# A graph-network pair kernel with 122 instead of 109 edge chunks sorted by cell, and the added source rows moved from TensorE to VectorE

## The reference, cut to what matters

```
h = relu(layernorm(x1 @ W1 + b1) * g1 + bt1)
edge_weights = sigmoid(relu(concat(h[src], h[dst]) @ We1 + be1) @ We2 + be2)
aggr = segment_sum(edge_weights[:, None] * h[src], dst, 6250)
gate = sigmoid(concat(h, aggr) @ Wg + bg)
out = layernorm(x1 + layernorm(gate * aggr + (1 - gate) * h) * g2 + bt2)
```

## Time and profile before

| | |
|---|---|
| median of 3 runs | 2032.33 us (2027.09 to 2037.23) |
| the profiled execution's own time | 2030.64 us |
| its span | 2028.9 us |
| mean granted TensorE clock | 0.905 |
| busy: PE / PEld / DVE / ACT / POOL | 87% / 69% / 77% / 66% / 68% |
| edge stage, node stage | 0 to 363 us, 363 to 524 us |
| gather stage: 26 steps without riders, 190 with | 524 to 785 us, 785 to 1937 us |
| end stage | 1937 to 2029 us |

### The profile page before, as it was taken

How to read it: one execution, slowest core, us unless ns; L and a number is a source line. 1 busy time by engine, 2 the same in 40 slices (tenths; PEclk the granted TensorE clock), 3 DMA queues, 4 the chain that set the end, 5 groups by cost and what they waited for, 6 DMA issues and landing times.

```text
span 2028.9 us, 42803 instructions
## 1 busy us (share of the span) xinstructions
PE 1762.4 (87%) x13262; PEld 1398.9 (69%) x13263; DVE 1560.1 (77%) x4602; ACT 1338.8 (66%) x3369; POOL 1375.0 (68%) x1415
## 2 busy tenths in 40 slices
PE   3899998667687789999999999999999999989880
PEld 2787777555465556666777778878887888778750
DVE  7877887596899657777788877778877887767766
ACT  1565555475655206778888878788877887767635
POOL 4564741167677777777777777777777777777736
PEclk9999998789678859898999999999998999999985
DMA  7898998415544455666666666777666677767502
GB/s 272 278 306 289 329 313 294 154 42 197 174 130 137 142 157 166 177 178 190 189 198 193 190 209 200 208 204 215 197 209 196 198 213 212 212 188 213 148 11 64
DMA packets 293551, 395.44 MB, mean 195 GB/s; under 512 B 73153, under 2 KB 195780, under 8 KB 293195
## 3 DMA queue, kind: packets, MB, share of 16 engines
q1 hardware_dynamic: 236559, 240.51, 37.6%
q0 software_dynamic: 54144, 147.92, 25.2%
q10 hardware_dynamic: 2620, 4.25, 0.6%
HBM read 377.32 MB, written 15.17 MB: 193 GB/s over the span
## 4 chain that ended last, share of the span: by engine, by line
PE 51%; POOL 24%; issue 11%; DVE 8%; DMA 3%; DVEq 1%; SPq 1%; ACT 1%; ACTq 0%; POOLq 0%
POOL x_rows L998 14%; PE psum L531 10%; PE psum L581 6%; PE psum L565 6%; POOL late_gathers L998 5%; POOL ring L998 5%; PE psum L1494 4%; PE psum L1495 4%; PE psum L1529 4%; PE psum L1506 4%; PE psum L1382 2%; PE psum L1537 2%; PE psum L560 2%; DVE stats L1869 1%; PE psum L1412 1%
## 5 line engine op out<-in xcount | busy, mean ns | idle before, releaser
L998 POOL DMA_INDIRECT x_rows<-src_table,lane_src x680 | 656.5, 966 | 216.0 <-issue 204.7
L585 DVE TENSOR_TENSOR sums<-sums,psum 128x128 f32 (+3 forms) x822 | 207.0, 252 | 181.2 <-issue 115.1
L576 DVE TENSOR_SCALAR weighted<-iota,lane_dst,weight 128x40 f32<-128x40 f32 x1128 | 262.4, 329 | 17.3 <-ACT weight L1205 17.2
L998 POOL DMA_INDIRECT late_gathers<-src_table,lane_src x224 | 217.0, 969 | 68.3 <-issue 67.6
L998 POOL DMA_INDIRECT ring<-src_table,lane_src x224 | 215.4, 962 | 68.3 <-issue 67.6
L531 PE MATMUL psum<-ring 128*64 128x128 f32 x3128 | 225.4, 288 | 35.3 <-issue 30.2
L565 PE MATMUL psum<-x_rows,ident 128*128 128x512 f32 x340 | 198.3, 677 | 46.0 <-DMA x_rows<-src_table,lane_src 46.0
L570 DVE SCALAR_TENSOR_TENSOR psum<-psum,we_all 128x512 f32<-128x512 f32 (+1 forms) x216 | 187.0, 866 | 50.5 <-PE psum L565 50.5
L531 PEld LDWEIGHTS psum<-ring 128*64 128x64 f32 x3128 | 177.6, 142 | 60.7 <-issue 42.8
L1217 ACT ACTIVATE sums<-psum 128x512 f32<-128x512 f32 (+1 forms) x149 | 87.4, 587 | 172.7 <-PE psum L1495 172.2
L572 DVE TENSOR_REDUCE logit<-psum 128x4 f32<-128x512 f32 (+1 forms) x216 | 184.6, 855 | 16.6 <-issue 0.8
(11 more groups left out here) (266 smaller groups left out, 3887.2 us busy)
## 6 DMA issues: line engine op xcount, KB each, us to landing
ring<-in_edge_attr SPq DMA_DIRECT2D x195, 512.0 KB, 5.3
ring<-cell_table SPq DMA_DIRECT2D x145, 256.0 KB
ring<-rel_table SPq DMA_DIRECT2D x70, 512.0 KB
ring<-src_table SPq DMA_DIRECT2D x192, 128.0 KB
x_rows<-src_table,lane_src POOLq DMA_INDIRECT x680
ring<-dst_table SPq DMA_DIRECT2D x282, 32.0 KB
ring<-src_table SPq DMA_DIRECT2D x106, 64.0 KB
src_table<-ring SPq DMA_DIRECT2D x12, 512.0 KB, 2.9
```

The costliest lines, as they stand in the source:

```text
L576: last = eng.tensor_scalar(out[:, j, :], iota1[:, 0:W], dst[:, j:j + 1], wt[:, j:j + 1], ALU.is_equal, ALU.mult)
L585: return eng.tensor_tensor(table[..., bass.ds(start, width)], table[..., bass.ds(start, width)], part, ALU.add)
L998: eng.indirect_dma_start(gathered(c)[:, j, :], None, src_table, bass.IndirectOffsetOnAxis(ap=lane_src[:, t:t + 1], axis=0)).then_inc(gathe ...
```

## The change

Thirteen more chunks (109 to 121) are sorted, as a sixth class with cap 2; 25 more riders follow from it (174 in all). The sort steps of classes 2 to 5 take 3 edge columns in place of 2. In every step with a rider (`vector_adds`), TensorE's `hidden_sum` does nothing; VectorE adds the gathered rows to the hidden rows in PSUM itself, ahead of L570. One of the three `place_dst` tiles is dropped, and `weigh_` waits with `PLACES` = 2. `far_onehot3` becomes a view of `node_hot`, and two PSUM result areas move.

```diff
-CLASSES = ((0, 41, 4), (41, 19, 2), (60, 19, 2), (79, 16, 2), (95, 14, 2))
+CLASSES = ((0, 41, 4), (41, 19, 2), (60, 19, 2), (79, 16, 2), (95, 14, 2), (109, 13, 2))
 
-SPANS = (80, 96, P, P, P)
-SORTED = 109
+SPANS = (80, 96, P, P, P, P)
+SORTED = 122
...
-        far_onehot3 = sb("far_onehot3", [P, J, WP], BF16)
...
-        SORT_STEPS = [9] + [2] * (n_classes - 1)
+        SORT_STEPS = [9, 2, 3, 3, 3, 3]
...
-        later_tiles = sort_tiles(SORT_STEPS[1], class_cells[1])
+        later_tiles = sort_tiles(max(SORT_STEPS[1:]), class_cells[1])
...
+        far_onehot3 = node_hot[:, 0, 0, 0:J * WP // 2].bitcast(BF16).rearrange("p (j w) -> p j w", j=J)
...
-        place_dst = [a.rearrange("p (k n) -> p k n", k=COLS) for a in (yard(RIDE), ring[:, behind_windows:behind_windows + RIDE], sb("place_dst", [P, RIDE])[:, :])]
+        place_dst = [a.rearrange("p (k n) -> p k n", k=COLS) for a in (ring[:, behind_windows:behind_windows + RIDE], sb("place_dst", [P, RIDE])[:, :])]
...
-            return const_bank[:, 320 + 16 * (i % 2):320 + 16 * (i % 2) + len(part_couples(i)) * n_classes]
-
-        totals_out = const_bank[:, 256:256 + 2 * n_couples * n_classes]
+            return const_bank[:, 320 + 32 * (i % 2):320 + 32 * (i % 2) + len(part_couples(i)) * n_classes]
+
+        totals_out = const_bank[:, 192:192 + 2 * n_couples * n_classes]
...
-        def dst_part(eng, out, hot_t, win):
+        def dst_part(eng, out, hot_t, win, whole=False):
...
-                last = eng.matmul(out[:, j, :], hot_t[:, j, :], win, start=(j == 0), stop=False, skip_group_check=True)
+                last = eng.matmul(out[:, j, :], hot_t[:, j, :], win, start=(j == 0), stop=whole, skip_group_check=True)
...
+        vector_adds = set(q for q in riders)
+
+        def pe_adds(q):
+
+            return sum(1 for p in range(q) if p not in vector_adds)
...
             def hidden_sum(q):
+                if q in vector_adds:
+                    return
...
             def logits(q):
-                need(eng, "hidden_sum", q)
                 need(eng, "weight", q - 4)
+                if q in vector_adds:
+                    need(eng, "hidden", q)
+                    for k, c in enumerate(step_chunks[q]):
+                        eng.wait_ge(gather_in[c % G_SLOTS], 16 * J * (c // G_SLOTS + 1))
+                        eng.tensor_tensor(hidden(q, k), hidden(q, k), gathered(c)[:, :, 0:P], ALU.add)
+                    eng.drain()
+                else:
+                    need(eng, "hidden_sum", pe_adds(q))
```

More of the change, by code:

```diff
@@ L447, in rank_out @@
         def rank_out(i):
-            return const_bank[:, 320 + 16 * (i % 2):320 + 16 * (i % 2) + len(part_couples(i)) * n_classes]
-        totals_out = const_bank[:, 256:256 + 2 * n_couples * n_classes]
-        assert 2 * n_couples * n_classes <= 256
+            return const_bank[:, 320 + 32 * (i % 2):320 + 32 * (i % 2) + len(part_couples(i)) * n_classes]
+        totals_out = const_bank[:, 192:192 + 2 * n_couples * n_classes]
+        assert 2 * n_couples * n_classes <= 308
         names = {}
@@ L1520, in hidden_mm @@
                         eng.wait_ge(*window_batch(c))
-                    last = dst_part(eng, hidden(q, k), onehot3_t[:, q % T_SLOTS, k, :, :], window[0:WP, c % Q_SLOTS, :])
+                    last = dst_part(eng, hidden(q, k), onehot3_t[:, q % T_SLOTS, k, :, :], window[0:WP, c % Q_SLOTS, :], q in vector_adds)
                 last.then_inc(done("hidden"), 1)
```

## The result

The changed kernel took 2265.98 us, median of 4 runs (2226.17 to 2288.26), against 2030.33 for the kernel before (4 runs, 2027.09 to 2037.23): a ratio of 1.1036 with an interval of 1.0971 to 1.1101. It is slower by 236 us, where +81 was forecast, and its time lies outside the range. The runs of this kernel scatter more than those of before; the median is of all four, while the ratio leaves out runs over 1.5% above the fastest, and by it the loss is 210 us. The profiled execution is the longest of the four, 2288.26 us with a span of 2286.6 and a mean granted clock of 0.827 (before: 0.905); it lies 22 us above the median.

What follows compares the result with a forecast made beforehand. The prediction took GpSimd's gathers to bound the stage with riders; longer rider steps would take it from 1152 to 1231 us (+79), the edge stage +2, so +81 on 2030.6: 2112 us, range 2035 to 2150.

Steps and rivals of the forecast that it cites:

- What bounds the kernel before: Stage with riders: GpSimd's gathers set the pace, 230 chunks of 5.0 us, 1150 of 1152 us.
- Gathers: GpSimd: 52 fewer gathers take 65 us off; with riders it then needs 1085 us.
- ScalarE's third column: ScalarE, rider steps with three sort columns: 6.75 us in place of 6.36, with nothing to hide it.
- VectorE's adds: VectorE, ahead of L570: 174 adds at a pitch of 0.76 us, 132 us in all.
- The bound with 0.84: Upper bound for a VectorE add: 0.84 us, with the 0.15 us standing before L585; 146 us in all.
- `PLACES` 2, the SyncE queue, the moved PSUM areas: Stage with riders: the `weigh_` wait, 25 more riders' loads on SyncE and the moved result areas each cost nothing.
- The fallback price: VectorE at L2011, if TensorE's `wsum` is not done in time: waits of 0.9 us for each of 25 riders.
- The sum of floors: Stage with riders: each step takes its longest floor, summing to 1231 us in place of 1152, +79.
- The step that failed: TensorE: removing 174 identity matmuls gains nothing in a rider step; the loop through ScalarE stays at 6.21 us.
- The rival "much slower": Sorting steps: TensorE waits about 1 us in each, clock falls to a mean of 0.85; 2165 us, chance 12%.
- the point of 0.91: TensorE's clock below which "much slower" decides: 5.15 / 5.69 = 0.91.
- What would show it: Signs, including GpSimd waiting at L581, adds of 0.69 us, unchanged TensorE loop, VectorE over 90% busy; wrong: clock under 0.9.

Runs made afterwards that it cites:

- the fourth experiment: Kernel before with three sort columns a step in classes 2 to 4 and two place tiles, TensorE still adding: 2618.76 us, 0.9999.
- the third set: Kernel before 2031.23 us; changed kernel unaltered 2238.32; changed kernel with TensorE adding 2100.36; changed kernel with an unneeded identity matmul on TensorE 2139.41.

## Why the prediction was right in sign and wrong in size

The steps of the prediction in turn, on the chips that take 2031 us for the kernel before, where nothing else is said:

- **What bounds the kernel before** was right: GpSimd's gathers. The exchange of relu and sigmoid left its time at 1.0004.
- **Gathers** were right in kind: 13 chunks fewer take GpSimd off the pace, and it waits for L581, as foretold. The 65 us bring nothing.
- **ScalarE's third column**: forecast 6.75 us for such a step, 6.77 in the timeline.
- **VectorE's adds**: forecast 0.76 at a base of 0.69; 102 of them average 708 ns, with a pitch of 0.77. The bound with 0.84 was not needed. The Trainium skill's flush after each operation ("VectorE: DVE Perf Modes", "The DRAIN you can't avoid"), taken as coming on top of the duration, would by an estimate make the pitch 1.1 us (the same section lets an operation that is not held start earlier); the trace shows 0.07 to 0.08 us between the end of an add and L570, so it did not appear as extra time here.
- **`PLACES` 2, the SyncE queue, the moved PSUM areas**: valued at nothing. None of the waits of L2019 is put down to L581, and the fourth experiment, which has two place tiles, gave 0.9999 (on a chip where other waits could hide a small cost). The fallback price read its row wrongly: of the 21.9 us idle before L2011 only 4.1 are a wait for the sigmoid, and 17.6 have no cause in the profile.
- **The sum of floors**, +79, assumed a clock of 1 for TensorE. Its own test is the kernel with everything but the moved adds: 2100.36 us, +69, and that kernel keeps its clock at 0.96 to 0.99. The sum is near, for a kernel that it was not made for, and in part by luck, as the next sentences show: it charges VectorE only in the 22 two-chunk steps, since in a rider step its 5.1 to 6.2 us lie under the loop and under ScalarE. (Counted over the trace of the changed kernel, VectorE's work is 5.12 us in a rider step and 6.20 with three columns, as forecast; in the two-chunk steps it is 5.4, 6.15 and 6.5 in place of 4.2, 4.9 and 5.3, a term too small by 1.2 us each, 26 us in all. The step read in the earlier trace rows as a two-chunk one has L570 and L572 on 512 elements, 0.69 us each, the logits of a one-chunk step; two chunks take 1.23 each, and their one-hot 0.13 more.) With that term put right the same sum gives some 1184 us for the kernel before, more than the 1152 measured, and 1257 for the changed one: "neither engine can bank a lead" is too strict, and in the forecast's 1231 this and the missing 26 us offset each other in part.
- **The step that failed** is "I give this **nothing** in a rider step: the loop through L1217 and L1209 stays at 6.21 without it", of the 174 identity matmuls. As time on TensorE they were in the shadow of ScalarE's part, as the earlier trace rows shows. But in that shadow they were what TensorE did while it waited. Without them it waits about 1 us in a step, the clock falls from 0.96 to 0.82, and "5.15 us on TensorE" is no longer 5.15: in 1014.8:1082.9, at 0.50, the relus are 10.0 to 10.4 us apart. The term put at nothing measured 138 us (2238 against 2100), and filling the hole again with a useless matmul gave 99 of them back.
- **By steps**, counted over the traces, mean us from one step to the next:

| step | forecast | changed | with filler | adds on TensorE |
|---|---|---|---|---|
| rider, no sorting (64) | 6.21 | 7.26 | 6.00 | 5.95 |
| rider, two columns (34) | 6.36 | 7.73 | 6.21 | 6.26 |
| rider, three columns (76) | 6.75 | 7.00 | 6.64 | 6.42 |

  The excess of the changed kernel over the forecast is 64 x 1.05 + 34 x 1.37 + 76 x 0.25 = 133 of the 175 us between 1231 and 1406; the rest, 42, is in the two-chunk steps, of which 26 are the term above. The engines work at several steps at once, so the table is coarse: counted from another instruction of the step, single entries move by up to 0.6 us, and the 133 to between 100 and 170. The three-column steps, which ScalarE was to pace, suffer least by every such count; that it is because TensorE has 1.3 us to spare in them is argued, not tested.

- **The rival "much slower"** named this mechanism, with the waits of about 1 us and the point of 0.91, and the profile after shows its sign (a clock under 0.9 in the sort stretch). It was held too unlikely at 12%, on the ground that the waits are shorter than those of 700:800, and priced too low at 2165. Its clock of 0.85 for the sorting steps was right as a mean: 785:1850 has 0.84, from 0.73 in the first 352 us to 0.92 in the last 350. But nothing was taken for the steps without sorting, where 1850:2100 has 0.75 and which by the table lose 1.05 us each, 67 us. What the price also left out is that the loss feeds itself: at the lower clock TensorE's part is longer, ScalarE and GpSimd wait longer for it (268 and 298 us in total, before 162 and 8.5), and TensorE then waits for them in its turn. The Trainium skill, "TensorE: Matmul & The Clock Gate", Part 1, which was cited with this rival, has the clock of an idle array dropped until it is busy again; the trace agrees with its two levels, 1.02 and 1.91 us for the same matmuls, and it sets in here with waits of 1 to 2 us a step.
- **What would show it**: the gathers off their pace, the waits for L581 and the add of 0.69 came as named. "VectorE over 90% busy" was wrong, it is 75%, and so was the unchanged loop, which is the step that failed. VectorE waits for the sigmoids (L2019, 105 us in 785:2100) like the others.

In sum, by the medians of the third set: +69 for the riders of the sixth class and the third column net of the gathers, +99 that a filler gives back, +39 for the adds on VectorE and what the filler did not bring back, together +207 on 2031. By the ratios it is 71 + 95 + 35, +202, and the result's own ratio gives +210; the two intervals overlap.

How the 99 us divide between the clock itself and the longer waits it causes cannot be told from these runs, since each brings the other. Nor was it tried how small a filler would do.

## What to carry to other kernels

Before you take an operation from TensorE because it costs nothing in its loop, ask what TensorE does in its place: if it waits, the granted clock may fall, and every matmul left pays. Test it with a matmul of the same shape that nothing needs; if the kernel with more work is faster, TensorE's idle time and the clock that goes with it were the price. And weigh a rider by what its step costs where it is the bound (6.2 us and more here): 25 more riders saved 13 chunks of 5.0 us of gathers, and cost, together with the third column, 69 us net.

## What the runs showed that was not expected

**A useless matmul is worth 99 us.** It has 306 records of 613 ns in the trace, and the kernel goes from 2238 to 2139 us. The waits beside which the clock falls are short, 0.9 us on average at L1480, on an engine that is busy for 90% of the time, and the longest of TensorE in the whole stretch is 2.4 us. The kernel before has waits of up to 5.5 us there (for a gather, at L565), but few, and keeps its clock at 0.96.

**Some chips are slower at this stage alone.** Two of the chips take 2586 and 2620 us for the kernel before, in place of 2030, with an edge stage of the same length. The trace there (kernel before with three columns, waits in 385:2500) gives `remote` as the releaser, that is, no instruction of this core:

```profile
ACT sums L1217 <- remote: 383.2, 78, 14.8
POOL x_rows L998 <- PE psum L581: 308.2, 43, 16.8
```

and its timeline shows one such pause:

```profile
842.45 0.39 PE L560 MATMUL psum<-ring,onehot_t 120*128 120x128 bf16 x4
...
850.61 0.95 POOL L998 DMA_INDIRECT ring<-src_table,lane_src  x1 [0.30 <-issue]
...
854.68 0.60 ACT L1217 ACTIVATE sums<-psum 128x512 f32<-128x512 f32 x1 [14.76 <-remote]
...
855.76 0.56 PE L1506 MATMUL psum<-we_col,sums 128*128 128x1 f32 x2 [12.92 <-ACT weight L1209]
```

For 12 us TensorE, ScalarE and VectorE all stand still. GpSimd goes on for seven gathers at 1.25 us each and stands still for the last 3.3. Then ScalarE and GpSimd begin within 0.2 us of each other and the others follow ScalarE; what held them the trace does not say, and it stays open. The clock is 0.81 around these pauses. On these two chips the changed kernel's loss is half (1.054, measured on one of them) and with the filler it is 1.0394 (on the other), so that little of the 4.7% that the filler is worth elsewhere is seen there; it was not run beside the changed kernel on the same one.
